# Prologue of a tuned kernel: text rows loaded in two pieces, patches in halves, rows of two batches computed directly, the order of loads and of GpSimd work changed

## The chip, the core and the metric

The kernel runs on one core of a Trainium2 chip. The metric is the device time in microseconds of one execution; the median of three runs stands for a kernel. The profile is of one further execution.

The engines are TensorE (PE in the rows; PEld is its loading of weights), VectorE (DVE), ScalarE (ACT), GpSimd (POOL) and SyncE (SP). SyncE only issues loads and stores here; ScalarE and GpSimd issue some too. An engine works through its own instructions in order and waits on semaphores for the others.

## What is computed

Eight images are cut into 36 patches of 768 numbers each and projected to 192; 128 rows of text follow them, so each of the 8 batches has 164 rows of 192. An attention with 12 heads and a routed feed-forward net of 16 experts are added. All is float32.

```
h = patches @ proj_w.T + proj_b + pos          # (8, 36, 192)
h = concat([h, txt], axis=1)                   # (8, 164, 192)
xn = layernorm(layernorm(h)) * ln_w
Q  = xn[:, None] * W_qk[None, :, None]         # 12 heads, Q is also K
A  = softmax(causal(Q @ Q.T / sqrt(192)))
o  = A @ (xn - mean(wte, axis=0))              # wte: 50257 x 192
h  = h + (o / row_number).reshape(8, 164, 12*192) @ W_o.T
h  = h + moe(layernorm(h))                     # top-1 of 16 experts, 64 rows each at most
```

The mean over the table wte (38.6 MB) is needed only at the end of the attention. The kernel adds the table up beside the attention.

## The kernel before

**Rows and batches.** Each batch of 164 rows is kept as 128 rows (36 patches and 92 of text, in H, row on partition) and 36 rows of text (in hB). Batch 0 has a stretch of its own before the loop. `iteration(b)` of every engine then finishes batch b and starts batch b + 1: TensorE computes the last two score groups of b (text rows, all heads), transposes z of b + 1, computes the values of b in four groups `value(b, 0..3)`, and between them the scores of b + 1 in groups `score(b+1, 0..2)` of 4 heads and the projection `project(b, ...)` of b with W_o. There are seven such iterations (0 to 6); behind them stand the last batch and the feed-forward part, which the change leaves alone.

**One batch on the other engines.** VectorE normalises: `variances` (BN stats), a power on GpSimd (`rsqrt`), a Newton step (`factors`), then `z(b)` makes zA and zB. TensorE transposes them, ScalarE copies the result (zT). GpSimd's `weigh` multiplies zT by the squared weights of each head into AwA (groups 0 to 2) and AwB (text rows, 3); for batch 0 ScalarE and VectorE make the halves with k = 0. After the scores VectorE takes row maxima (`row_max`), ScalarE the exponentials (`exps`), VectorE a factor per row (`row_factor`), and GpSimd multiplies (`normalise`). TensorE transposes P, ScalarE copies it to a rounded high part (`t_copy`), VectorE makes the rest (`t_low`), and the values use both. `value_low` does the same for z. `o_copy` and `e_copy` empty the value banks, `residual` adds the projection to H.

**The prologue.** SyncE loads the projection weights, the patches, the text rows (txtA, partitions 36 to 127, in one load), waits for these and for some constants, and then issues wo_attn, the first two chunks of wte, txtBp and further loads. ScalarE's queue carries the constants: cst, txtB, position and bias, wqk, lnw and then lncol, flnw, wrt and flc. TensorE keeps warm with 14 products of ones, computes embT = patches^T for batches 0 and 1 first (`embed`, in bT[1]), ScalarE copies it, and `token_transpose(j)` gives the patch rows of two batches at a time; VectorE's `add_patches(j)` adds the position and writes H. Then follow the other six batches in the same way, with 12 more warming products around the transposes of z.

**The table.** 28 chunks of 1.34 MB. Six are loaded plain by SyncE (`plain_loads`, one per batch) and summed by VectorE (`plain_sum`). The other 22 go through two buffers: the first two by plain loads, the other 20 by loads that add in memory, which GpSimd issues (`add_wte`), three per iteration for iterations 0 to 5. `add_wte` waits until the earlier load into its buffer has landed. Everything that GpSimd has to do after it waits too. In the loop, the three adds stand before the weighing of groups 0 and 1, before that of group 2, and before `normalise(b+1, (1,))`.

**Order.** It is written by hand on every engine; there is no planner. `mat` is a set of constants that ScalarE converts to bfloat16 after its iteration 1 and TensorE uses after batch 7.

## Time and profile before

| | us |
|---|---|
| median of three runs | 373.03 (372.75 to 373.41) |
| the profiled execution | 372.14 |
| its span | 370.4 |
| TensorE busy in the span | 332.7 (90%) |
| VectorE, GpSimd, ScalarE busy | 219.9, 169.0, 127.9 |

The span is cut into the prologue (up to 37.8 us, where TensorE transposes z of batch 1), batch 0 (to 71.6), the loop, and from 203 us the end of the attention and the experts. TensorE is the busiest engine, so its idle stretches are where to look; in the chain of work that ended last TensorE has 39%, loads 14% and GpSimd 14% of the span.

In a row of the timeline the columns are: start in us, duration in us, engine, line of the kernel, operation, what is written <- what is read, shape, and in brackets how long the engine stood idle before it and who ended that. "x16" means that 16 instructions are merged in the row. One float32 matmul shows as two.

### The profile page before, as it was taken

To read this page: it belongs to the slowest core of one execution; us is meant where nothing else is said; L and a number is where in the kernel's file an instruction comes from. 1 tells how busy PE (TensorE), PEld (TensorE's weight loads), DVE (VectorE), ACT (ScalarE), POOL (GpSimd) and SP (SyncE) were. 2 spreads that over 40 slices of the span, in tenths; PEclk is the share of its full clock that TensorE was granted. 3 is DMA by queue.
4 is the path that set the end of the run, shared out by engine and by line. 5 is a ranking of instruction groups with operands and counts; after the bars stand their busy time and mean duration, and the time that the engine had idled before them with its cause. 6 is when DMAs were issued, how large, how long until landed. Compare 5 with 4: busy or idle time off the path is not lost.

```text
span 370.4 us, 6796 instructions
## 1 busy us (share of the span) xinstructions
PE 332.7 (90%) x2352; PEld 306.4 (83%) x2352; DVE 219.9 (59%) x546; ACT 127.9 (35%) x438; POOL 169.0 (46%) x181
## 2 busy tenths in 40 slices
PE   5886779999799899899899898999949999999992
PEld 1866679989699799799798798999824999999991
DVE  1479638678669679578588888656476222222221
ACT  2065423644643453454436004545720111111110
POOL 3067375583574763862953501450562134444321
PEclk9899889999999999999999999999998999999997
DMA  7399999899799899799797999900223599999930
GB/s 226 114 419 341 215 213 212 236 177 210 221 196 213 225 199 239 191 199 271 162 198 155 295 229 237 230 11 0 84 101 93 165 276 276 273 265 272 273 93 15
DMA packets 20176, 74.29 MB, mean 201 GB/s; under 512 B 3388, under 2 KB 9021, under 8 KB 18874
## 3 DMA queue, kind: packets, MB, share of 16 engines
q0 software_dynamic: 7344, 30.57, 40.8%
q1 hardware_dynamic: 9898, 40.40, 36.8%
q10 hardware_dynamic: 2912, 3.04, 2.9%
q8 instruction: 12, 0.20, 0.2%
q14 instruction: 10, 0.08, 0.1%
HBM read 66.12 MB, written 9.25 MB: 203 GB/s over the span
## 4 chain that ended last, share of the span: by engine, by line
PE 39%; issue 18%; DMA 14%; POOL 14%; DVE 8%; ACT 3%; POOLq 1%; SPq 0%; DVEq 0%; ACTq 0%
PE bO L1198 18%; DMA wbuf<-in_wte 11%; PE bE L1198 10%; PE bS L1198 5%; PE bJ L1198 4%; POOL AwA L390 4%; DMA H<-in_txtA 4%; POOL PA L416 3%; POOL wbuf L401 3%; POOL AwB L390 2%; ACT PA L552 2%; POOL PB L416 1%; DVE negmax L791 1%; PE bT L1544 1%; DVE PTB0L L808 1%
## 5 line engine op out<-in xcount | busy, mean ns | idle before, releaser
L552 ACT ACTIVATE PA<-bS,negmax 128x128 f32<-128x128 f32 x96 | 33.9, 366 | 85.2 <-DVE negmax L791 85.2
L416 POOL TENSOR_TENSOR PA<-PA,rn 128x512 f32<-128x512 f32 x24 | 25.8, 1075 | 64.3 <-DVE rn L803 64.3
L390 POOL TENSOR_TENSOR AwA<-zT,w 96x512 f32<-96x512 f32 x45 | 53.4, 1514 | 3.3 <-ACT zT L534 3.3
L1198 PE MATMUL bJ<-wo_sb,oTA 128*128 128x192 f32 x288 | 51.4, 328 | 0.0
L1198 PEld LDWEIGHTS bS<-zT,AwA 96*128 96x128 f32 x384 | 48.0, 197 | 1.1
L1198 PE MATMUL bS<-zT,AwA 96*128 96x128 f32 x384 | 48.2, 280 | 0.0
L1198 PEld LDWEIGHTS bJ<-wo_sb,oTA 128*128 128x128 f32 x288 | 46.2, 190 | 0.0
L1198 PE MATMUL bO<-PA,wx 96*128 96x112 f32 x384 | 45.4, 275 | 0.5 <-DVE PA L1171 0.5
L1198 PEld LDWEIGHTS bO<-PA,wx 96*128 96x128 f32 x384 | 44.9, 192 | 0.7 <-DVE PA L1171 0.7
L463 POOL DMA_INDIRECT out<-PA,yrow x16 | 15.0, 940 | 56.1 <-DVE PA L1187 56.1
L689 ACT ACTIVATE AwA<-bO 128x448 f32<-128x448 f32 x16 | 8.7, 543 | 78.4 <-PE bO L1198 52.8
L1198 PE MATMUL bE<-wx,AwA 128*112 128x192 f32 x192 | 33.9, 326 | 0.0
L827 DVE TENSOR_REDUCE wx<-wx 128x672 f32 (+1 forms) x24 | 31.5, 1314 | 0.0
L401 POOL DMA_DIRECT2D wbuf<-in_wte x20 | 27.3, 1363 | 7.7 <-DMA wbuf<-in_wte 6.2
L1198 PEld LDWEIGHTS bE<-wx,AwA 128*112 128x112 f32 x192 | 30.4, 177 | 0.0
L1180 DVE TENSOR_SCALAR AwA<-bO 128x224 f32<-128x224 f32 x16 | 6.3, 391 | 36.7 <-PE bO L1198 34.5
L791 DVE TENSOR_REDUCE negmax<-bS 128x4 f32<-128x512 f32 x24 | 16.5, 687 | 13.7 <-PE bS L1198 13.5
L416 POOL TENSOR_TENSOR PB<-PB,rn 108x328 f32<-108x328 f32 x16 | 11.7, 733 | 28.1 <-DVE rn L803 27.3
L570 ACT ACTIVATE oTA<-bO,lncol 128x512 f32<-128x512 f32 x24 | 16.6, 690 | 13.0 <-PE bO L1198 12.9
L1198 PE MATMUL bS<-zT,AwB 96*108 96x164 f32 x128 | 20.3, 302 | 0.0
L458 POOL DMA_INDIRECT dispatched<-pay,posI x11 | 12.3, 1122 | 16.3 <-ACT pay L616 12.1
L552 ACT ACTIVATION_READ_ACCUMULATOR PA<-bS,negmax 128x1 f32 x96 | 19.5, 203 | 0.0
(247 smaller groups left out, 690.9 us busy)
## 6 DMA issues: line engine op xcount, KB each, us to landing
wbuf<-in_wte POOLq DMA_DIRECT2D x20, 1344.0 KB, 13.0
wx<-in_wi SPq DMA_DIRECT2D x16, 576.0 KB
wx<-in_wo SPq DMA_DIRECT2D x16, 576.0 KB
wx<-in_wte SPq DMA_DIRECT2D x6, 1344.0 KB, 8.5
dispatched<-zeros SPq DMA_DIRECT2D x7, 675.5 KB, 10.3
wbuf<-in_wte SPq DMA_DIRECT2D x2, 1344.0 KB, 12.1
AwA<-dispatched ACTq DMA_DIRECT2D x14, 168.9 KB
wo_sb<-in_wo_attn SPq DMA_DIRECT2D x1, 1728.0 KB, 6.9
```

The source lines that it names most:

```text
L390: nc.gpsimd.tensor_tensor(o, zT[:, k, ss].unsqueeze(1).to_broadcast(list(o.shape)), w2[:, k, hs].unsqueeze(2).to_broadcast(list(o.shape)), ...
L401: pool.dma_start(wchunk[s], wv[:, ds(c, 1), :].rearrange("p c x -> p (c x)"), accum_op=ALU.add, max_dma_last_dim=WR * EMB * 4 // 2).then_i ...
L416: nc.gpsimd.tensor_tensor(t, t, q.unsqueeze(2).to_broadcast(list(t.shape)), ALU.mult).then_inc(p_ready, 1)
L458: nc.gpsimd.indirect_dma_start(out=xd[:, :], out_offset=bass.IndirectOffsetOnAxis(ap=posI[0:n, j:j + 1], axis=0), in_=pay[0:n, j, :], in_o ...
L463: nc.gpsimd.indirect_dma_start(out=out[:, :], out_offset=bass.IndirectOffsetOnAxis(ap=idx, axis=0), in_=rows, in_offset=None, bounds_check ...
L552: last = nc.scalar.activation(PA[:, h, :], bank[:, j * SA:(j + 1) * SA], ACT.Exp, bias=negmax[:, h:h + 1], accum_out=lsum[:, h:h + 1])
L570: nc.scalar.activation(dst, src, ACT.Copy, scale=lncol[:, 0:1]).then_inc(o_used, 1)
L689: nc.scalar.activation(hT[:, 0:4, :], bO[0][:, 0:4 * T].rearrange("p (c n) -> p c n", c=4), ACT.Relu).then_inc(h0_ready, 1)
L791: nc.vector.tensor_reduce(negmax[:, 4 * r:4 * r + 4], bS[r % 2][:, :].rearrange("p (h s) -> p h s", h=4), X, ALU.max, negate=True).then_in ...
L827: nc.vector.tensor_reduce(psums.rearrange("p (n e) -> p n e", e=EMB)[:, ds(b, 1), q].rearrange("p n e -> p (n e)"), plain.rearrange("p (r ...
L1180: nc.vector.tensor_scalar(hT[:, 4:6, :], bO[1][:, 0:2 * T].rearrange("p (c n) -> p c n", c=2), 0.0, None, ALU.max).then_inc(h1_ready, 1)
L1198: return nc.tensor.matmul(o, l, r, start=start, stop=stop, skip_group_check=True)
```

## The change

- The text rows of txtA are loaded as 80 and 12 partitions instead of 92; txtBp is loaded right behind them, before SyncE waits.
- Patches and projection weights come in two halves of three slices each (pat_in, pat2_in), to other buffers (parts of wx[1] and wx[3]), as does embT.
- Rows of batches 0 and 1 are computed directly (`embed_rows`, patches x weights); the other six go by `embed` and `token_transpose` as before, the second half of `embed` after the transposes of z of batch 0 and the transposes after score groups 0 and 1. The 12 warming products there are gone.
- SyncE also waits for w2 and ln; the first two table chunks are issued before wo_attn, and mat is loaded after all plain chunks. ScalarE issues its late constants after the patches have landed, and converts mat in iteration 6.
- VectorE's variances and factors of batches 2 to 7, and three of the adds of patches, move back into and behind the scores of batch 0.
- GpSimd weighs z of the next batch (groups 0 and 1) before the first add of an iteration; the second add comes after `normalise(b+1, (0,))`, the third after the weighing of the text rows. Iterations 0 and 1 stand outside its loop.

```diff
-            sp.dma_start(pw_sb, projw).then_inc(pat_in, 16)
-            sp.dma_start(pat_sb, patches).then_inc(pat_in, 16)
-            sp.dma_start(H[IMG:128, 0:NBATCH, :], txtA).then_inc(txt_in, 16)
+            for part, arrived in ((slice(0, 3), pat_in), (slice(3, 6), pat2_in)):
+                sp.dma_start(pw_sb[:, part, :], projw[:, part, :]).then_inc(arrived, 16)
+                sp.dma_start(pat_sb[:, part, :], patches[:, part, :]).then_inc(arrived, 16)
+            for p0, p1 in ((IMG, 116), (116, 128)):
+                sp.dma_start(H[p0:p1, 0:NBATCH, :], txtA[p0 - IMG:p1 - IMG]).then_inc(txt_in, 16)
+            sp.dma_start(H[0:BP, NBATCH:SLOTS, :], txtBp).then_inc(late_in, 16)
...
-            sp.wait_ge(txt_in, 16)
-            sp.dma_start(wo_sb[:, :, :], wo_attn).then_inc(wo_in, 16)
+            sp.wait_ge(w_in, 32)
+            sp.wait_ge(txt_in, 32)
             for s in range(WBUF):
                 sp.dma_start(wchunk[s], wv[:, s, :]).then_inc(wte_first, 16)
-            sp.dma_start(H[0:BP, NBATCH:SLOTS, :], txtBp).then_inc(late_in, 16)
+            sp.dma_start(wo_sb[:, :, :], wo_attn).then_inc(wo_in, 16)
...
+            plain_loads(sp)
             sp.dma_start(mat32, cst2_d[:, C_MAT:NCST2]).then_inc(mat_in, 16)
-            plain_loads(sp)
...
             pool.wait_ge(w2_ready, 1)
-            weigh(0, 1, (1,), range(3))
-            rsqrt(rstd[:, :, 2:NBATCH], nmr[:, :, 2:NBATCH], 2)
-            weigh(0, 1, (1,), (3,))
-            normalise(0, range(1))
+            weigh(0, 1, (1,))
             add_wte(2, 0, 0)
-            normalise(0, range(1, 2))
             add_wte(3, 1, 0)
-            normalise(0, range(2, 3))
+            normalise(0, range(3))
...
                 normalise(b, range(3, SPR))
-                for k in range(4):
-                    if r is not None and k < 3:
-                        add_wte_nth(i, r + k)
-                    if k == 0:
-                        weigh(b + 1, t_before(b, "z") + 1, (0, 1), (0, 1))
-                    elif k == 1:
-                        weigh(b + 1, t_before(b, "z") + 1, (0, 1), (2,))
-                        normalise(b + 1, (0,))
-                    elif k == 2:
-                        normalise(b + 1, (1,))
-                        weigh(b + 1, t_before(b, "z") + 1, (0, 1), (3,))
-                    else:
-                        normalise(b + 1, (2,))
+                n = t_before(b, "z") + 1
+                weigh(b + 1, n, (0, 1), (0, 1))
+                if r is not None:
+                    add_wte_nth(i, r)
+                weigh(b + 1, n, (0, 1), (2,))
+                normalise(b + 1, (0,))
+                if is0(b):
+                    rsqrt(rstd[:, :, 2:NBATCH], nmr[:, :, 2:NBATCH], 2)
+                if r is not None:
+                    add_wte_nth(i, r + 1)
+                normalise(b + 1, (1,))
+                weigh(b + 1, n, (0, 1), (3,))
+                if r is not None:
+                    add_wte_nth(i, r + 2)
+                normalise(b + 1, (2,))
...
             dve.wait_ge(vz_ready, 3)
             z(0)
-            for j in range(1, 4):
-                add_patches(j)
-            variances(2, NBATCH)
-            row_max(0, 0)
             dve.wait_ge(t_used, 1)
             nc.vector.tensor_tensor(AwB[:, 0, :, :], ...)
+            row_max(0, 0)
             row_max(0, 1)
             row_factor(0, 0)
-            value_low(0)
+            for j in range(2, 5):
+                add_patches(j)
             row_factor(0, 1)
             row_max(0, 2)
+            value_low(0)
             dve.wait_ge(t_ready, 1)
             z(1)
             row_factor(0, 2)
-            factors(2, NBATCH, 2)
...
                 e_copy(b, 2)
+                if is0(b):
+                    variances(2, NBATCH)
                 plain_sum(b, 0)
...
                 dve.wait_ge(t_ready, t_before(b, "z") + 1)
+                if is0(b):
+                    factors(2, NBATCH, 2)
                 z(b + 2)
...
-            embed(bT[1][0:EC, 0:EF], 0, 0, EF)
-            embed(bT[1][0:EC, 128:128 + EF], 1, 0, EF).then_inc(emb_ready, 1)
+            embed_rows(0, 0, 3)
+            embed_rows(1, 0, 3)
+            pe.wait_ge(pat2_in, 32)
+            embed_rows(0, 3, 6)
+            embed_rows(1, 3, 6)
             embed(bO[0][0:EC, EF:NBATCH * IMG], 0, EF, NBATCH * IMG).then_inc(emb_ready, 1)
...
-            stay_warm(bS[0], 6)
             z_transpose(0, 0)
-            stay_warm(bS[0], 6)
+            embed(bO[1][0:EC, EF:NBATCH * IMG], 1, EF, NBATCH * IMG).then_inc(emb_ready, 1)
             pe.wait_ge(bf_ready, 3)
-            for r in range(3):
-                score(0, r, r < 2)
+            score(0, 0, True)
+            score(0, 1, True)
+            pe.wait_ge(embT_ready, 2)
+            for j in range(1, 4):
+                token_transpose(j)
+            score(0, 2)
```

## Rows read from the trace of the kernel before

**Rows 1.** Stretches: busy time of each engine, granted clock, DMA share, GB/s.
```profile
71.60:98.40 26.80, 25.15 (x179) 23.30 (x178) 19.57 (x38) 14.07 (x49) 16.08 (x18) 1.00 0.94 205
98.40:124.50 26.10, 24.39 (x175) 22.77 (x174) 19.30 (x37) 11.84 (x47) 15.96 (x16) 1.00 0.95 211
```

**Rows 2.** Chain of work in order of time; then one stretch as in rows 1.
```profile
1.76 13.91 DMA H<-in_txtA
...
10.00:11.00 1.00, 0.78 (x9) 0.79 (x10) 0.97 (x10) 0.00 (x0) 0.00 (x0) 1.00 0.26 106
```

**Rows 3.** Timeline of the prologue, TensorE and VectorE; then one load, KB, landing.
```profile
10.22 3.26 PE L1198 MATMUL bT<-AwA 128*96 128x72 f32 x24 [4.29 <-DMA AwA<-in_patches]
...
13.83 0.18 DVE L757 TENSOR_TENSOR w<-w,ln 96x24 f32<-96x24 f32 x1 [2.50 <-DMA ln<-in_lnw]
...
16.69 0.55 DVE L743 TENSOR_TENSOR H<-bT,cS 36x384 f32<-36x384 f32 x1 [2.25 <-PE bT L1219]
...
20.83 0.37 DVE L785 TENSOR_SCALAR zB<-hB,rstd,nmr 36x192 f32<-36x192 f32 x1
...
ln<-in_lnw ACTq DMA_DIRECT2D x1, 0.8 KB, 10.3
```

**Rows 4.** Timeline from the first scores to the transposes of z(1).
```profile
22.87 1.66 DVE L763 BATCH_NORM_STATS2 st<-H 128x6 f32<-128x192 f32 x6
...
26.33 0.69 DVE L791 TENSOR_REDUCE negmax<-bS 128x4 f32<-128x512 f32 x1 [0.47 <-PE bS L1198]
...
31.86 2.30 DVE L783 TENSOR_SCALAR zA<-H,rstd,nmr 128x192 f32<-128x192 f32 x1
...
33.34 1.76 POOL L401 DMA_DIRECT2D wbuf<-in_wte  x1
...
34.09 0.36 DVE L785 TENSOR_SCALAR zB<-hB,rstd,nmr 36x192 f32<-36x192 f32 x1
...
34.71 0.17 DVE L730 TENSOR_TENSOR nwz<-rstd 128x12 f32<-128x12 f32 x1
...
36.86 0.19 DVE L886 TENSOR_TENSOR wr_sb<-wr_sb,flc 96x32 f32<-96x32 f32 x1
...
37.84 0.32 PE L1241 MATMUL bT<-cst,zA 128*96 128x128 f32 x1 [1.96 <-DVE PTAL L808]
```

**Rows 5.** Timeline of iteration 0, GpSimd, TensorE, VectorE; last the score of iteration 1.
```profile
44.92 1.21 POOL L401 DMA_DIRECT2D wbuf<-in_wte  x1 [3.12 <-DMA wbuf<-in_wte]
...
48.29 0.38 PE L1198 MATMUL bS<-maskA,idb 128*128 128x512 bf16 x1 [3.37 <-issue]
48.50 3.37 PE L1198 MATMUL bS<-zT,AwA 96*128 96x128 f32 x16
...
51.91 0.69 DVE L791 TENSOR_REDUCE negmax<-bS 128x4 f32<-128x512 f32 x1 [5.28 <-PE bS L1198]
...
75.19 1.95 PE L1198 MATMUL bS<-zT,AwA 96*128 96x128 f32 x16
```

**Rows 6.** One iteration of the loop; then a wait: us, times, longest.
```profile
124.50 1.20 POOL L401 DMA_DIRECT2D wbuf<-in_wte  x1
125.27 4.49 POOL L390 TENSOR_TENSOR AwA<-zT,w 96x512 f32<-96x512 f32 x4
...
136.99 2.12 PE L1198 MATMUL bJ<-wo_sb,oTA 128*128 128x192 f32 x12
...
PE bS L1198 <- POOL AwA L390: 4.1, 5, 0.9
```

**Rows 7.** Timeline of ScalarE in the second iteration.
```profile
91.18 1.92 ACT L608 ACTIVATE mat<-pay 128x2048 bf16<-128x2048 f32 x1
```

**Rows 8.** GpSimd's normalising and third add; then the adding loads, us to landing.
```profile
118.62 1.04 POOL L416 TENSOR_TENSOR PA<-PA,rn 128x512 f32<-128x512 f32 x1 [3.73 <-DVE rn L803]
...
134.98 1.21 POOL L401 DMA_DIRECT2D wbuf<-in_wte  x1
...
wbuf<-in_wte POOLq DMA_DIRECT2D x20, 1344.0 KB, 13.0
```

73 lines of the change are left out of this document (37 added, 36 removed).

## The prediction

> **What bounds the kernel now.** I read three views, in this order. First the busy time by stage [rows 1]: in a batch of the running loop (98.4 to 124.5 us) TensorE is busy 24.39 of 26.10 us, so the loop goes at TensorE's pace but for 1.7 us. Then the chain of waits from the start, with the DMA share beside it [rows 2]: the first long link is the load of the text rows, issued at 1.76 and landed at 15.67, while in 10 to 11 us (and alike up to 15) the 16 DMA engines are at 0.26 of their time, 106 GB/s. That is four engines' worth; one load is still under way on a quarter of them. Last the waits of each engine in batch 0 and in the loop [rows 3 to 6]. The end of the run is set by TensorE from batch 1 on, so what counts is (a) how early TensorE gets through batch 0 and (b) each hole it has in the loop.
>
> The working is in old times: a term is how much earlier TensorE's stream stands against its old place. It is made against the profiled execution, 372.14 us with a span of 370.4; the 1.74 around the span stay, and the median of the runs, 373.03, is 0.9 above it, so the gain is taken from 373.03 at the end.
>
> **Term 1, up to z of batch 0.** Now: the patches (one load) let TensorE start at 10.22, it makes embT for two batches, ScalarE copies it, four transposes give the rows, VectorE adds the position at 16.69, and zB ends at 20.83 + 0.37 = 21.20 [rows 3]. The direct product patches x weights needs no copy and no transposes. It is 12 matmuls with 192 columns; such matmuls take 0.33 us each in the loop (six of them, 12 halves in the profile, in 2.12 us, [rows 6]), so 4.0 us at the full clock, half of it on the first three slices, which come in before the second half. The second half is the end of the same 1.44 MB and lands about when the patches land now, 10.2, or somewhat before, since the late constants of ScalarE's queue (109 KB) now wait behind it and the text no longer shares its engines: I take 9.8. Then six matmuls, 2.0 us: rows of batch 0 at 10.8, of batch 1 at 11.8. The text (480 KB on 80 partitions) follows at the rate of a full set of engines: 106 GB/s x 4 for 480 + 72 KB is 1.3 us, so about 11.2. What is late next is VectorE: it is idle 2.50 us for the load ln and makes w at 13.83 [rows 3]. If ln still lands then, VectorE reaches the two adds at 14.43, ends them (two of 0.4) at 15.2, and z ends 3.95 later as now (17.24 to 21.20), at 19.2: gain 2.0. If ln lands with the rest at 11.3, adds end at 12.6 and z at 16.6: gain 4.6. A load of 0.8 KB that takes 10.3 us while its neighbours in the queue take 5 to 7 is held up by something on its engines, and the text load is the only thing there until 15.67; I take 4.0, ends 2.0 and 4.8.
> The Trainium skill (DMA: Bandwidth & Descriptors, "Why a DMA increments its semaphore by 16 and not by 1") says that a load is spread over the largest number up to 16 that divides its partitions, and that its semaphore write comes after all earlier writes of the same engine. By it 92 rows use 4 engines, 80 use 16, 12 use 12, and ln waits behind the text; the 0.26 share agrees, and the sum by it would be 4.6 instead of 4.0.
>
> **Term 2, from z to the transposes of z of batch 1 (21.20 to 37.84, [rows 4]).** On VectorE 2.99 us of variances (22.87 to 25.86, where the wait of 0.47 before the first row maximum begins) leave their place, worth nothing there because of that wait. The block between z(1) and the first t_low, 34.71 to 37.05, moves into and behind batch 0: 2.3 us, on the path, because TensorE waits 1.96 us at 37.84 for exactly that t_low. Added: the three adds of patches (0.55 each, 1.7) between row maximum 1 and row maximum 2. Between the exponentials of a row group VectorE waits for ScalarE, which hides most of them; I put 0.3; the copy emb_copy(1) on ScalarE costs 0.35 before the first exponentials. The second embed product (2.2 us full clock, 4 at half) stands before the first score, which comes 2.0 us after the z transposes anyway for want of weighed z: 0.2 to 2. GpSimd's four weighings run on without the power of the other batches in between, and its first adds of the table no longer wait with a row in front: the two chunks come ahead of wo_attn, issued about 12.5 instead of 16.1, 2.9 MB at 0.4 MB/us, in by about 21.5, about when GpSimd comes to them. And zA(1), 2.30 us beside GpSimd's work, may be 0.4 or stay. Sum: 2.3 + up to 1.9 - 0.3 - 0.35 - 0.2 to 2: 0.5 to 3; I take 2.0.
>
> **Term 3, the first values (37.84 to 44.92).** TensorE runs there at half speed after its idle stretch: a score of 16 halves right after the hole takes 3.37, in the loop 1.95 [rows 5]. Without the 1.96 us hole the same work takes some 5.6 instead of 7.1: 1.4 (0 to 1.6).
>
> **Term 4, the hole before the score of batch 1.** GpSimd waits 3.12 us for a table chunk (41.80 to 44.92) before it issues the add; only then does it weigh z, and TensorE idles 3.37 us until 48.29 [rows 5]. With the weighing in front it starts at 41.8 and is done with the first group 2.0 us later, in these old times at 43.8 and earlier still with the terms above: the whole hole goes, and 1.42 us of slow clock on the score, together 4.8, up to the value of the last group. But the variances of six batches, 2.99 us, now stand on VectorE between the last e_copy and the row maximum of batch 1; so far VectorE had 5.28 us to spare there, which the hole gave it [rows 5]. Without the hole: e_copy ends at x, variances x + 3.0, plain_sum 1.3, maximum 0.7, exponentials 1.5, two copies and differences of P 1.9: x + 8.4, whereas TensorE, leaving its score at x + 1, gets to that value at x + 5.5 or so. It waits 2.9 there, a new hole. Net 4.8 - 2.9 = 1.9 (0.9 to 4.7). After such a hole the clock falls again, now on the stretch behind it: -0.8 (0 to -1.6), in which the factors of the other batches (2.4 with a slow step) are too; they stand before z(2), and its row maximum had 2 us of slack to the end of the batch.
>
> **Term 5, the loop.** In a batch the add is issued at 124.50 and the weighing starts 0.77 later, at 125.27; TensorE waits 0.8 for the weighed z, 4.1 us in 5 batches [rows 6]. With the add behind the first four weighings 0.77 of it goes: 5 x 0.75 = 3.8 (0 to 4.1). The moved adds: the second stays at its place, the third goes behind the weighing of the text rows, just where VectorE makes z(b+2). TensorE's other waits of 0.2 to 0.3 stay. Term 6: the conversion of mat, 1.92 us on ScalarE [rows 7], made its batch 26.8 us long instead of 26.1 [rows 1]; in its new place ScalarE is idle: 0.65 (0 to 0.7). Its load of 1 MB goes behind the last plain chunk, tens of us ahead of its use; the table's last chunks get some 3 us later by it. From there to the end nothing moves but by the shift.
>
> **Sum:** 4.0 + 2.0 + 1.4 + 1.9 - 0.8 + 3.8 + 0.65 = 12.95; 373.03 - 12.95 = 360.1. All lower ends give 1.8, all upper ones 18.9; they don't fall together.
>
> **Rival A: the moved add costs VectorE what TensorE gains (the loop gives 0).** The chain into TensorE's 0.80 wait runs through VectorE without slack: e_copy, value_low, z, maxima, t_low, exponentials, GpSimd's normalising. Two-source operations of VectorE stretch when GpSimd is at work: zA took 2.30, where zB with the same columns takes 0.36, in a stretch with an add and a normalising [rows 4]. If an add of 1.2 us does that alone, z is 0.7 later and the 0.77 are given back: 12.95 - 3.8 = 9.2, 363.9. Against it: zB at 34.09 took its usual 0.36 while an add was being issued (33.34 to 35.10) [rows 4].
> The Trainium skill (SBUF — State Buffer, the box on "DVE blocks DMA") tells of one port pair of VectorE and GpSimd which is locked for a whole instruction, descriptors of GpSimd's DMAs included. Taken both ways it is this rival, 363.9; the row of zB speaks against it, that of zA for it.
>
> **Rival B: the prologue gives little.** ln or the 12 rows still land near 13.8, and TensorE, with its warming matmuls gone, falls to half clock before the z transposes: term 1 is 2.0, term 2 is 0.5 to 1: 12.95 - 2.0 - 1.3 = 9.7, 363.4. For it: TensorE idled 4.29 us before 10.22 [rows 3] and would be idle some 3 before z. If splitting the text doesn't do what it says at all (both pieces land at 15.7) term 1 is 0.5: 365.
>
> **Rival C, slower: GpSimd stuck behind the table.** The third add follows the first, into the same buffer, by 12.5 us (now 10.5), and behind it stands the normalising of the third round, on which TensorE's transposes wait; GpSimd is idle 3.73 us before it [rows 8], and TensorE comes to it about 3 us after it is done, by my reading of the order. An add lands 13.0 us after its issue [rows 8]; the DMA share of a batch is 0.95 [rows 1] and batches get shorter, so it may grow. Above 19.2 us each further one costs six batches 1 us: slower than before from 21.4 us on; at 23 it is 22.8 - 12.95 = 10 slower, 383. Against it: the bytes of a batch stay the same, and now the third add follows the first after 10.5 us (134.98 less 124.50) without a wait for it.
>
> **Chances.** As forecast 0.60 (356 to 363), A 0.15, B 0.17 (both 361 to 367), text split without effect 0.04, C 0.03, no change 0.01. The range 355.5 to 367.0 holds the first three but for their edges, some 0.85. About 0.2% is what a measurement here tells from no change. Faster 0.96, same 0.01, slower 0.03.
>
> **What the new profile would show.** Text landed near 11, w made near 12, z(0) finished near 17; the transposes of z(1) near 32; no wait of TensorE for weighed z in batch 0, but 2 to 3 us before its last value; "TensorE waits for GpSimd's weighed z" near 0.2 us in all, VectorE's zA in the loop about 0.4 (else A); a batch of 25.4 us without exception; the loop's end 12 to 13 us earlier and the rest unchanged. A wrong size of the hole in batch 0 and the clock behind it is what is likeliest to spoil the number.

## The result, and the profile after

| | us |
|---|---|
| before, median beside these runs | 373.22 |
| after, median of four runs | 377.16 (372.82, 376.93, 377.40, 382.04) |
| ratio to before | 1.008 (95%: 1.005 to 1.012) |
| forecast | 360.1 (355.5 to 367.0) |
| the profiled execution of after, its span | 372.82, 371.0 |

The change makes the kernel slower by 0.8%, where 12.95 us of gain were forecast. The run of 382.04 fell in a slower state of the chip; the ratio and all medians below leave such runs out, which makes this one 376.93. The profiled execution is the shortest of the four; v1_after_again below shows what a longer one loses.

From the page of after: TensorE's busy time, and the shares of the chain of work that ended last:

```profile
PE 333.8 (90%) x2336; PEld 305.3 (82%) x2336; DVE 218.3 (59%) x547; ACT 126.4 (34%) x437; POOL 167.9 (45%) x181
...
PE 46%; DVE 21%; DMA 18%; ACT 7%; issue 5%; ACTq 1%; DVEq 1%; POOLq 0%; POOL 0%
```

TensorE is busy about as long as before (332.7 us), so what was to be gained is still in its idle stretches and in matmuls at a lower clock. GpSimd, with 14% of the chain in before, has left it, and 15% of the span are now one kind of load, the plain chunks of the table (`DMA wx<-in_wte`).

The waits of after between 60 and 205 us (who waited for whom, us in total, times, longest) hold two that before has not:

```profile
DVE wx L833 <- DMA wx<-in_wte: 8.2, 5, 2.0
PE bO L1206 <- DVE PTB1L L814: 8.0, 5, 2.0
```

TensorE's wait for GpSimd's weighed z [rows 6] is gone, as forecast. In its place VectorE waits in every iteration for the plain chunk of the table, and TensorE, for as long, for VectorE. The reason is in the tile of that load. First before, then after (us from issue to landing):

```profile
DMA to landing us min/median/max: 7.6/8.4/9.4
```
```profile
DMA to landing us min/median/max: 11.1/11.3/11.7
```

The chain of work that ended last, in after, from the first to the second of these loads:

```profile
61.87 1.24 DVE wx L833
63.12 11.07 DMA wx<-in_wte
...
75.60 0.69 DVE negmax L797
...
87.72 0.59 DVE negmax L797
88.32 1.25 DVE wx L833
89.58 11.26 DMA wx<-in_wte
```

This is a ring, a closed loop through one buffer. SyncE issues the next load only when VectorE has summed the last quarter of the chunk before (88.32 + 1.25), and VectorE can't go on in the next batch before the load has landed. In the next batch the first quarter starts at 100.99 and the last ends at 116.2, 15.2 us later. With 11.4 us from issue to first use the ring is 26.65 us long, and this is what an iteration takes (26.70 on average). GpSimd's timeline of after shows the pace at the normalising of the text rows, once per iteration:

```profile
68.43 1.57 POOL L420 TENSOR_TENSOR PB<-PB,rn 108x328 f32<-108x328 f32 x2 [3.43 <-DVE rn L809]
94.77 1.57 POOL L420 TENSOR_TENSOR PB<-PB,rn 108x328 f32<-108x328 f32 x2 [3.32 <-DVE rn L809]
...
201.93 1.57 POOL L420 TENSOR_TENSOR PB<-PB,rn 108x328 f32<-108x328 f32 x2 [3.33 <-DVE rn L809]
```

The same rows of before stand at 69.86 and 201.53. I use this event as a clock below and call it "text rows of batch 1" (68.43) and "of batch 6" (201.93). So after enters the loop 1.43 us earlier than before, and leaves it 0.40 later: 133.50 us for five iterations instead of 131.67.

The prologue, TensorE and VectorE of after:

```profile
13.56 0.18 DVE L762 TENSOR_TENSOR w<-w,ln 96x24 f32<-96x24 f32 x1 [3.86 <-DMA ln<-in_lnw]
18.39 0.37 DVE L791 TENSOR_SCALAR zB<-hB,rstd,nmr 36x192 f32<-36x192 f32 x1
33.99 0.27 PE L1252 MATMUL bT<-cst,zA 128*96 128x128 f32 x1
40.21 0.39 PE L1206 MATMUL bS<-maskA,idb 128*128 128x512 bf16 x1
```

And iteration 0 of after, in which the lead that the prologue has won is lost (VectorE, then TensorE):

```profile
40.80 1.65 DVE L768 BATCH_NORM_STATS2 st<-H 128x6 f32<-128x192 f32 x6
42.49 0.51 DVE L771 BATCH_NORM_AGGREGATE mv<-st 128x2 f32<-128x6 f32 x6
43.03 2.00 DVE L773 TENSOR_SCALAR nmr<-mv 128x12 f32<-128x12 f32 x1
...
49.71 0.59 DVE L814 TENSOR_TENSOR PTB1L<-bT,PTB1H 36x432 fp32r<-36x432 f32 x1
```
```profile
50.45 0.70 PE L1206 MATMUL bO<-PTB0H,vAH 128*128 128x432 f32 x1 [4.00 <-DVE PTB1L L814]
...
55.27 2.63 PE L1206 MATMUL bJ<-wo_sb,oTA 128*128 128x192 f32 x12
```

The score of batch 1 starts at 40.21 without a wait; in before it is at 48.29 [rows 5], 8.1 us later. Before the last group of values (50.45) TensorE stands idle for 4.00 us, and the 12 projection halves behind that take 2.63 us instead of 2.12.

### The profile page after: what moved, and what is told of

Its sections match the earlier page's. It is cut to its first block, busy times and chain, and to the rows that moved or that the text cites. A ratio compares the mean times of both kernels' runs of the same rounds, so it can differ in the third digit from the quotient of the medians.

```text
span 371.0 us, 6757 instructions
## 1 busy us (share of the span) xinstructions
PE 333.8 (90%) x2336; PEld 305.3 (82%) x2336; DVE 218.3 (59%) x547; ACT 126.4 (34%) x437; POOL 167.9 (45%) x181
## 4 chain that ended last, share of the span: by engine, by line
PE 46%; DVE 21%; DMA 18%; ACT 7%; issue 5%; ACTq 1%; DVEq 1%; POOLq 0%; POOL 0%
PE bO L1206 21%; DMA wx<-in_wte 15%; PE bE L1206 12%; PE bJ L1206 6%; PE bS L1206 4%; ACT PA L557 3%; DMA ln<-in_lnw 3%; DVE negmax L797 2%; DVE wx L833 2%; DVE vAL L826 2%; DVE vBL L824 2%; DVE vBL L826 1%; DVE PTB0L L814 1%; DVE PTB1L L814 1%; DVE PTAL L814 1%
## 5 line engine op out<-in xcount | busy, mean ns | idle before, releaser
L420 POOL TENSOR_TENSOR PA<-PA,rn 128x512 f32<-128x512 f32 x24 | 24.8, 1034 | 77.8 <-DVE rn L809 77.8
L394 POOL TENSOR_TENSOR AwA<-zT,w 96x512 f32<-96x512 f32 x45 | 48.4, 1161 | 3.5 <-ACT zT L539 3.5
L1206 PEld LDWEIGHTS bS<-zT,AwA 96*128 96x128 f32 x384 | 46.8, 192 | 1.2
L1206 PE MATMUL bS<-zT,AwA 96*128 96x128 f32 x384 | 46.8, 275 | 0.0
L405 POOL DMA_DIRECT2D wbuf<-in_wte x20 | 24.1, 1230 | 0.0
## 6 DMA issues: line engine op xcount, KB each, us to landing
wbuf<-in_wte POOLq DMA_DIRECT2D x20, 1344.0 KB, 11.2
wx<-in_wi SPq DMA_DIRECT2D x16, 576.0 KB, 11.5
wx<-in_wte SPq DMA_DIRECT2D x6, 1344.0 KB, 11.3
wo_sb<-in_wo_attn SPq DMA_DIRECT2D x1, 1728.0 KB, 12.3
```

What stands on the lines that cost most here:

```text
L394: nc.gpsimd.tensor_tensor(o, zT[:, k, ss].unsqueeze(1).to_broadcast(list(o.shape)), w2[:, k, hs].unsqueeze(2).to_broadcast(list(o.shape)), ...
L405: pool.dma_start(wchunk[s], wv[:, ds(c, 1), :].rearrange("p c x -> p (c x)"), accum_op=ALU.add, max_dma_last_dim=WR * EMB * 4 // 2).then_i ...
L420: nc.gpsimd.tensor_tensor(t, t, q.unsqueeze(2).to_broadcast(list(t.shape)), ALU.mult).then_inc(p_ready, 1)
L1206: return nc.tensor.matmul(o, l, r, start=start, stop=stop, skip_group_check=True)
```

## Experiments on the ring (the loop)

**Theory.** The ring of one buffer sets the pace of after. It does so because the third add of the table now stands close in front of the plain load (issued at 86.44, the plain load at 89.58; in before they are some 9 us apart, 82.15 and 91.0) and shares the DMA engines with it. **Rivals.** VectorE stretched by adds (rival A), or contention for bytes that no buffer cures.

**x1_two_plain.** After, with two buffers for plain chunks in turn:

```diff
-        plain = wx[0][:, :]
+        plain = (wx[0][:, :], wx[2][:, :])
...
-                    if n:
-                        sp.wait_ge(plain_used, 4 * n)
-                    sp.dma_start(plain, ...).then_inc(plain_in, 16)
+                    if n > 1:
+                        sp.wait_ge(plain_used, 4 * (n - 1))
+                    sp.dma_start(plain[n % 2], ...).then_inc(plain_in[n % 2], 16)
```

> The changed kernel, but with two buffers for the plain chunks of the table (the second in wx[2]), so that a chunk is loaded a batch ahead; VectorE's loop is written out in pairs for that. Theory T (the moved adds lengthen the plain load from 8.4 to 11.3 us, and VectorE waits 8.2 us for it in 5 iterations, with TensorE behind it): the wait is gone, an iteration takes 25.1 us instead of 26.7, and the time is 373 - 8 = 365 (363 to 367). Rival R (the loads as such are the bound, any gain before them is given back there): the wait moves to GpSimd's adds or to the end of the table, an iteration stays above 26, and the time is 370 to 375.

Measured: 364.66, ratio to before 0.981 (0.976 to 0.987). Its waits have no row for the plain chunk, though the loads take as long as in after:

```profile
DMA to landing us min/median/max: 11.4/11.5/11.7
```
```profile
68.10 1.57 POOL L421 TENSOR_TENSOR PB<-PB,rn 108x328 f32<-108x328 f32 x2 [3.30 <-DVE rn L810]
...
194.84 1.57 POOL L421 TENSOR_TENSOR PB<-PB,rn 108x328 f32<-108x328 f32 x2 [3.32 <-DVE rn L810]
```

126.74 us for five iterations, 25.35 each. The loads are as slow as before, only the wait goes. Between the profiled executions (372.82 and 364.87) this gives 8.0 us, of which 6.8 are in these five iterations; between the medians it is 12 us, measured on two chips (10 by the two ratios to before). In this loop the first quarter is wanted 9.8 us after the last one of the batch before is done (88.17 to 97.94). That is what a ring of one buffer allows for the load at this pace; a load of 11.4 us exceeds it by 1.6, and 5 times 1.6 is about the 8.2 us of the wait.

**x3_before_third.** The kernel before, with nothing but the third add moved behind the weighing of the text rows (from k = 2 to k = 3):

```diff
-                    if r is not None and k < 3:
-                        add_wte_nth(i, r + k)
+                    if r is not None and k != 2:
+                        add_wte_nth(i, r + min(k, 2))
```

> The kernel before with one thing moved: the third add of each iteration goes from before the normalising of round 1 to behind the weighing of the text rows. Theory T: the plain load takes 10.5 to 11.5 us instead of 8.4, VectorE waits for it 1 to 1.5 us in each of 5 iterations, 26.7 us an iteration: 373.2 + 2.5 = 375.7 (374.5 to 378). Rival R: a place in the order changes nothing, 373.

Measured: 375.58, ratio 1.009 (1.006 to 1.013).

```profile
DVE wx L827 <- DMA wx<-in_wte: 2.9, 4, 1.9
```
```profile
DMA to landing us min/median/max: 9.9/10.1/10.9
```

The place of this one add, which I had costed at nothing, is enough: the plain load lands 1.7 us later, VectorE waits, and the kernel before becomes some 3 us slower (375.58 against 372.44 beside it; in the profile five iterations take 133.43 us instead of 131.67). It doesn't explain all of the 11.3 us in after. There the second add is later too (80.28, 9.3 us before the plain load; in before 14.7), so that by the median time to landing (11.2 us; in before 13.3) two adds are under way when the plain load is issued, where in before it is one. What this is worth wasn't tried by itself.

**x2_old_adds.** After, with the adds of iterations 1 to 5 back in front of the weighings:

```diff
+                if r is not None and not is0(b):
+                    add_wte_nth(i, r)
                 weigh(b + 1, n, (0, 1), (0, 1))
                 if r is not None:
-                    add_wte_nth(i, r)
+                    add_wte_nth(i, r if is0(b) else r + 1)
                 weigh(b + 1, n, (0, 1), (2,))
                 normalise(b + 1, (0,))
...
-                    add_wte_nth(i, r + 1)
+                    add_wte_nth(i, r + 1 if is0(b) else r + 2)
...
-                if r is not None:
+                if r is not None and is0(b):
                     add_wte_nth(i, r + 2)
```

> The changed kernel with the adds of iterations 1 to 5 back in their old places; iteration 0 keeps the weighing in front. Theory T: plain load 8.4 us, no wait of VectorE, an iteration of 26.15 us as before; the 3.0 us that TensorE has gained at the end of iteration 0 and 0.65 of the conversion stay: 369.5 (368.5 to 371). Rival R: no different from the changed kernel, 373 to 377.

Measured: 372.05, ratio 0.997 (0.994 to 1.001). The plain loads land in 8.1 to 8.3 us but for the first (11.6), which follows iteration 0 with its third add in the new place. The old wait is back,

```profile
PE bS L1208 <- POOL AwA L394: 4.3, 5, 1.0
```

and an iteration takes 26.3 us. The mechanism is as expected, the time 2.6 above my figure of 369.5. Iteration 0 has the same hole of 4.00 us as in after (text rows of batch 1 at 68.62), and of the 1.45 us by which the profiled execution leaves the loop earlier than before (200.08) nothing is left at its end; where they go stands behind y3_text_one, at the end of the experiments.

**x4_one_first.** After, with the adds one weighing earlier each, so that the third is issued well ahead of the plain load (the conditions `if r is not None` are left out here):

```diff
-                weigh(b + 1, n, (0, 1), (0, 1))
+                weigh(b + 1, n, (0, 1), (0,))
                 add_wte_nth(i, r)
+                weigh(b + 1, n, (0, 1), (1,))
+                add_wte_nth(i, r + 1)
                 weigh(b + 1, n, (0, 1), (2,))
                 normalise(b + 1, (0,))
-                add_wte_nth(i, r + 1)
+                add_wte_nth(i, r + 2)
                 normalise(b + 1, (1,))
                 weigh(b + 1, n, (0, 1), (3,))
-                add_wte_nth(i, r + 2)
```

> The changed kernel with another order on GpSimd, in all iterations: weigh group 0, add, weigh group 1, add, weigh group 2, normalise round 0, add, normalise round 1, weigh the text rows, normalise round 2; that is before's order but for one weighing ahead of the first add. Theory T: the adds are as early against the plain load as in the kernel before, it lands in 8 to 9 us, VectorE doesn't wait, TensorE has the first group 0.77 us earlier: 25.3 us an iteration and 364 to 367 in all. Rival R: 370 to 375. Should the gain of the loop come from nothing but the adds' place, this equals the run with two plain buffers within 1.5 us.

Measured: 369.52, ratio 0.993 (0.990 to 0.997), above the 364 to 367 expected. The plain loads land in 8.2 us, so that wait is gone, but another engine now waits:

```profile
POOL wbuf L405 <- DMA wbuf<-in_wte: 14.5, 5, 3.0
```

This is rival C of the prediction in a mild form: the third add (105.44) comes before the first one, into the same buffer (94.89), has landed, and GpSimd stands in front of it for 2.9 us with its normalising behind. An iteration takes 26.4 us. So of the two orders tried, one is too early (GpSimd waits) and one too late (the plain load is late): the old places were a compromise with 1.9 us of slack (10.3 us from the last use of the buffer to the next first one, less 8.4 of load).

**z3_before_plain.** The kernel before with two plain buffers, nothing else:

> The kernel before with two plain buffers in turn, and nothing else. Theory (the second buffer only takes away a wait that the new order of GpSimd makes; before, VectorE does not wait for plain loads): same as before, 372.6, with 26.1 us an iteration. Rival (the second buffer gives something by itself, since the plain load can go at any time): 369 or less, with under 25.6 us an iteration.

Measured: 375.66, ratio 1.007 (1.005 to 1.010). The loop keeps 26.3 us an iteration (131.46 us for five, before 131.67), near what was expected, but the kernel is 3 us slower, which I had not. The place is the first add of iteration 0, in [rows 5] after 3.12 us of waiting; GpSimd in z3_before_plain:

```profile
48.07 1.21 POOL L402 DMA_DIRECT2D wbuf<-in_wte  x1 [5.95 <-DMA wbuf<-in_wte]
```

A second plain chunk (1.34 MB) is now asked for at the start, ahead of the load that GpSimd waits for. That load, issued at 31.82, takes over 15 us instead of 12.8; the add is 3.2 us later than in before (48.07, 44.92), the text rows of batch 1 are 4.2 later (74.02, 69.86), and those of batch 6 are 4.0 later (205.48). Before that load the prologue is at most 0.5 us late (31.82, in before 31.36), so the second chunk is the likely cause; it wasn't tried alone. A second buffer isn't free where an engine waits for the loads that it overtakes.

**y4_before_pool_plain.** z3_before_plain with the new order of GpSimd's iterations; the prologue is that of before:

> The kernel before with GpSimd's new order in the iterations and two plain buffers, and nothing of the prologue changed. Theory T: the loop gives 5 x 0.75 and batch 0 the hole of 3.37 us and some slow clock: 372.4 - 3.8 - 4 = 364.6 (363 to 367), so that nearly all that the changed kernel with two buffers gains comes from this and little from the prologue. If the prologue carried it instead: 368 to 371.

Measured: 365.21, ratio 0.979 (0.975 to 0.983), as the theory had it; text rows of batch 1 at 65.74, of batch 6 at 193.02. The late table chunk no longer matters, since the weighing stands in front of the add. With this order and two buffers the new prologue adds next to nothing (364.66 against 365.21). By the text rows it even loses: x1_two_plain has them at 68.10 and 194.84, 2.4 and 1.8 us later than here. The next section asks why.

**v1_after_again.** The kernel after, unchanged, on another chip.

> The kernel after once more, on another chip, beside the kernel before. Its four times were 372.82 (the profiled one), 376.93, 377.40 and 382.04, so the profile shows the shortest of them, and what the others lost has not been seen. Theory (the ring of one plain buffer sets the pace, and its length hangs on how long a plain load takes to land beside the adds): median between 375 and 378; in a profiled execution of some 377 the iteration is 27.2 to 27.5 us instead of 26.7 and the plain loads land in about 12 us. Rival (the loop is the same and the time is lost at the end, in the experts): iterations of 26.7, and the experts' stretch 4 us longer.

Measured: 376.37, ratio 1.011 (1.008 to 1.014), as the theory had it; the profiled execution took 375.19. Its chain:

```profile
116.28 1.24 DVE wx L834
117.54 12.26 DMA wx<-in_wte
...
143.90 1.25 DVE wx L834
145.17 11.80 DMA wx<-in_wte
```

The plain loads take 11.5 to 12.3 us, VectorE waits 10.4 us for them, and five iterations take 137.27 us, 27.45 each, against 26.70 in the first profile of after. The text rows of batch 6 come 2.5 us later, the whole execution is 2.4 us longer. So this longer run loses its time in the loop, where the ring is: once a load is on the path, its spread is the kernel's. (The first of the five iterations takes 28.45 us; in it TensorE also runs at a granted clock of 0.66 from 79 to 84 us, behind a hole of 1.78.) The runs of 377 and more weren't profiled.

## Experiments on the prologue and iteration 0

**z2_prologue_only.** After, with GpSimd's iterations (0 included) in the order of before, one plain buffer:

```diff
-                weigh(b + 1, n, (0, 1), (0, 1))
-                if r is not None:
-                    add_wte_nth(i, r)
...
+                for k in range(4):
+                    if r is not None and k < 3:
+                        add_wte_nth(i, r + k)
```

> The kernel after, but in its iterations GpSimd has the order of the kernel before again (each add in front of a weighing or a normalising), with one plain buffer. It says what the prologue of the change is worth by itself. Theory (y4_before_pool_plain against x1_two_plain: the prologue is worth less than 1 us): 372 to 373.3 beside 373. The last plain loads land in 8.5 us, GpSimd's wait for the table chunk in batch 0 and TensorE's hole of 3 us behind it are back. Rival (the prologue's 3 us of earlier TensorE work, seen in the kernel after, come through once the loop does not take them back): 369 to 370.

Measured: 368.52, ratio 0.990 (0.985 to 0.995), nearest to the rival and somewhat below its 369: by itself the prologue, with the new place of mat, is worth 4.2 us. TensorE and GpSimd in iteration 0:

```profile
49.50 0.44 PE L1206 MATMUL bO<-PTB0H,vAH 128*128 128x432 f32 x1 [1.11 <-DVE PTB1L L814]
```
```profile
65.73 1.57 POOL L420 TENSOR_TENSOR PB<-PB,rn 108x328 f32<-108x328 f32 x2 [3.43 <-DVE rn L809]
```

The hole before the value is 1.11 us instead of 4.00, no slow clock behind it, and batch 1 is there at 65.73, 2.7 us earlier than in after, although its score starts 2.0 later (42.17). x2_old_adds differs from this kernel in iteration 0 alone: 68.62 and 372.05. The new order in iteration 0, which I had counted as the end of a hole, costs about 3 us beside the new place of the variances (2.9 by the text rows, 3.5 by the medians).

**y1_var_late.** x1_two_plain, with the variances and their power later in iteration 0:

```diff
             def iteration(b, par, turn):          # VectorE
...
                 e_copy(b, 2)
-                if is0(b):
-                    variances(2, NBATCH)
                 plain_sum(b, 0, par, turn)
...
                 plain_sum(b, 2, par, turn)
+                if is0(b):
+                    variances(2, NBATCH)
...
                 normalise(b + 1, (0,))            # GpSimd
-                if is0(b):
-                    rsqrt(rstd[:, :, 2:NBATCH], nmr[:, :, 2:NBATCH], 2)
...
                 normalise(b + 1, (1,))
+                if is0(b):
+                    rsqrt(rstd[:, :, 2:NBATCH], nmr[:, :, 2:NBATCH], 2)
```

> Changed kernel with two plain buffers, and the variances of batches 2 to 7 (4.2 us on VectorE there, 40.8 to 45.0) moved from before the row maximum of batch 1 to before the last e_copy of batch 0, where VectorE waits 3.4 us for TensorE; GpSimd's power goes behind the normalising of round 1. Theory V (the variances make TensorE's hole of 4.00 us in batch 0 and the 2.3 us of half clock behind it): hole under 1 us, batch 1 starts 4 to 6 us earlier, 364.7 - 5 = 360 (358.5 to 362). Rival (VectorE's chain up to the start of batch 1 gives it back): the hole goes, but the first loop iteration starts no earlier, 364.

Measured: 364.52, ratio 0.980 (0.976 to 0.984). This is the rival's time, but not what the rival said would happen. The hole of 4.34 us in x1_two_plain is gone (0.26 is left), and batch 1 does come earlier, by 3.0 us:

```profile
65.06 1.57 POOL L421 TENSOR_TENSOR PB<-PB,rn 108x328 f32<-108x328 f32 x2 [3.30 <-DVE rn L810]
```

It isn't the 4 to 6 us of the theory, since in the waits of 40 to 62 us stands

```profile
DVE nwz L735 <- POOL rstd L384: 2.1, 1, 2.1
```

VectorE now waits for the power before z(2), and TensorE as long for the exponentials (2.29 us at 60.21). At the end of the loop 1.9 of the 3.0 us are left (192.92 against 194.84). All but 0.2 of these go behind the loop, where the 26 warming products ahead of the experts run at a granted clock that differs from profile to profile. First x1_two_plain, then y1_var_late:

```profile
271.24 5.78 PE L1209 MATMUL bJ<-ones 128*128 128x512 bf16 x26 [1.51 <-DVE nbI L1165]
```
```profile
269.30 8.37 PE L1209 MATMUL bJ<-ones 128*128 128x512 bf16 x26 [1.50 <-DVE nbI L1165]
```

That the two kernels take the same time (364.87 and 364.66 in their profiles) is thus an accident of the clock there, and no sign that the variances don't matter.

**z1_best.** y1_var_late, with the power in its old place again, and VectorE's product of the router's weights taken from behind iteration 0 to where VectorE has time:

```diff
                 normalise(b + 1, (0,))            # GpSimd
+                if is0(b):
+                    rsqrt(rstd[:, :, 2:NBATCH], nmr[:, :, 2:NBATCH], 2)
...
                 plain_sum(b, 1, par, turn)        # VectorE
+                if is0(b):
+                    dve.wait_ge(late_in, 16 * 5)
+                    link(nc.vector.tensor_tensor(wr_sb[:, :, :], ...))
```

> The kernel after, with the two plain buffers of x1_two_plain; VectorE's variances of batches 2 to 7 stand before the last e_copy of batch 0 as in y1_var_late, but GpSimd takes their power ahead of the first normalising of batch 1, and VectorE scales the router's weights one step later. Theory (what y1_var_late lost was VectorE's wait of 2.15 us for the power): that wait goes, batch 1 starts some 1.5 to 2 us earlier than in x1_two_plain, which had 364.66, and this stays to the end of the loop: 361.5, between 360 and 363.5. Rival (time won in batch 0 is given back at the end, where the experts' first blocks wait for work that does not move): 364.5, with the warming products of 8 us or more ahead of the experts, as in y1_var_late.

Measured: 361.70, ratio 0.970 (0.966 to 0.974), the fastest of all and 4% under the kernel after; the theory had 361.5.

```profile
64.54 1.57 POOL L421 TENSOR_TENSOR PB<-PB,rn 108x328 f32<-108x328 f32 x2 [2.18 <-DVE rn L810]
...
191.19 1.57 POOL L421 TENSOR_TENSOR PB<-PB,rn 108x328 f32<-108x328 f32 x2 [3.32 <-DVE rn L810]
```

VectorE's wait for the power is 1.17 us instead of 2.15, not quite gone. Batch 1 is there 3.6 us earlier than in x1_two_plain, of which y1_var_late already had 3.0. The variances in the wrong place are what had eaten most of the prologue's gain. In the right place the prologue is worth 3.5 us beside the new order too (against the 365.21 of y4_before_pool_plain); in the profiled executions 1.8 of this are there at the text rows of batch 6 (191.19, 193.02), and the other 1.8 are in the warming products (7.11 and 8.64 us) and just ahead of them.

**v2_iter0_old.** x1_two_plain, with the adds in the old places in iteration 0 alone:

```diff
+                if is0(b):
+                    add_wte_nth(i, r)
                 weigh(b + 1, n, (0, 1), (0, 1))
+                if is0(b):
+                    add_wte_nth(i, r + 1)
                 weigh(b + 1, n, (0, 1), (2,))
                 normalise(b + 1, (0,))
+                if is0(b):
+                    add_wte_nth(i, r + 2)
```

> The kernel x1_two_plain (after with two plain buffers), but in iteration 0 alone GpSimd has its adds in the old places, in front of the weighings. x1_two_plain had 364.66, with 4.34 us of hole before the value of batch 0 and the text rows' normalising of batch 1 at 68.10; z2_prologue_only, with the old places everywhere, has 1.11 us of hole, and that normalising at 65.73. Theory (the new order in iteration 0 brings TensorE's score early and so makes a long hole behind it, which lowers the clock; with an add in front there are two short ones): the normalising at 65.7, then 25.4 us an iteration, 362.3, between 361.5 and 363.5. Rival (the earlier start is lost in the tail or to the table's chunks, which GpSimd now has to wait for in batch 1): 364 to 365.

Measured: 367.53, ratio 0.986 (0.982 to 0.990), text rows of batch 1 at 70.20 instead of 65.7. Neither case holds: the add in front of the weighing waits, as in z3_before_plain, for a load that the second plain chunk stands ahead of:

```profile
42.23 1.20 POOL L406 DMA_DIRECT2D wbuf<-in_wte  x1 [2.95 <-DMA wbuf<-in_wte]
```

In z2_prologue_only, with one plain buffer, that wait is 0.79. The second buffer and the old order don't go together in iteration 0, the new order and the early variances don't either; of the combinations tried z1_best has the good one.

## Experiments on the loads of the prologue

**y2_ln_first.** x1_two_plain, with w2 and ln issued first on ScalarE's queue (in the diff, ahead of cst):

```diff
+            for dst, src in ((w2[:], wqk), (ln96[:], lnw)):
+                act.dma_start(dst, src).then_inc(w_in, 16)
```

> Changed kernel with two plain buffers, and ScalarE issues the two small loads w and ln first instead of fifth and sixth. In the changed kernel VectorE waits 3.86 us for ln (until 13.47) and SyncE's table loads wait for it as well. Theory L (ln is late because it stands behind other transfers): it lands by 8, z of batch 0 is done near 17.2 instead of 18.8, 364.7 - 1.5 = 363.2. Rival (a load of 8 byte pieces takes its 10 us wherever it stands, or its end is reported only when the engines are empty): ln lands after 11, 364.7.

Measured: 366.71, worse by 2 than the 364.66 of x1_two_plain. The first step of theory L holds: ln lands 3.8 us after its issue instead of 10.1, and VectorE no longer waits for it. But the other loads come later. VectorE begins with the text rows of hB at 11.63 instead of 6.59, and TensorE waits for the second half of the patches,

```profile
12.41 1.82 PE L1209 MATMUL bT<-wx 128*36 128x192 f32 x5 [4.16 <-DMA wx<-in_patches]
```

and zB starts at 19.93 instead of 18.53. So the times of both cases fall, and with them the rival's claim that ln takes 10 us wherever it stands.

**y3_text_one.** x1_two_plain, with the text rows in one load of 92 partitions:

```diff
-            for p0, p1 in ((IMG, 116), (116, 128)):
+            for p0, p1 in ((IMG, 128),):
```

> Changed kernel with two plain buffers, and the text rows in one load of 92 partitions as in the kernel before. Shows what the split is worth. If the split is what brings the text early (theory): it lands near 15.5 instead of before 13, z of batch 0 is 0.7 to 1.5 later, and 364.7 + 1 = 365.7. If the gain of the prologue is from elsewhere: 364.7.

Measured: 367.6, worse by 3 than x1_two_plain, of which the profile shows 0.8 at z (zB at 19.37 instead of 18.53). VectorE's timeline:

```profile
11.86 0.18 DVE L763 TENSOR_TENSOR w<-w,ln 96x24 f32<-96x24 f32 x1 [1.99 <-DMA ln<-in_lnw]
...
15.81 0.62 DVE L769 BATCH_NORM_STATS2 st<-H 128x6 f32<-128x192 f32 x2 [2.71 <-DMA H<-in_txtA]
```

The text is what is late (15.8), as in [rows 2], and VectorE has ln 1.8 us earlier than with the text split (11.86 here, 13.69 in x1_two_plain). So splitting the text moves ln back, where the forecast had it come forward. The Trainium skill (DMA: Bandwidth & Descriptors, "Queues, rings and completion order") says that a load's semaphore write lands only after every earlier write of the same DMA engine. The forecast read from it that ln waits for the whole text load; the trace doesn't agree with that reading, for ln is used at 11.86 here and at 13.83 in before, while the text lands at 15.8 and 15.67. Which of the other writes ln waits for, no run here shows.

**What lies behind the loop.** The profiled executions settle where the rest of these 2 and 3 us goes. From the text rows of batch 6 to the 26 warming products it is 76.4 us in x1_two_plain, y1_var_late, y2_ln_first, y3_text_one and z1_best alike (76.6 in y4_before_pool_plain), and from the end of these products to the end of the run 87.0 to 87.9. The products themselves take 5.78, 8.37, 7.07, 8.39, 7.11 and 8.64 us. In y3_text_one this makes 1.9 of the 3.2 us that its profile is longer, in y2_ln_first 0.4 of 1.1; the loop's end is 1.3 and 0.7 us later. The same products take 8.36 us in x2_old_adds and 7.20 in before. A difference of a us or two between two medians can thus come from there, and the text rows are the better measure of what a change in the prologue is worth.

## Why the prediction was wrong, step by step

Against [rows 3 to 6], in the profiled execution of after:

| term | forecast | measured | seen at |
|---|---|---|---|
| 1, z of batch 0 | 4.0 (2.0 to 4.8) | 2.44 | end of zB: 21.20, now 18.76 |
| 2, to the transposes of z(1) | 2.0 (0.5 to 3) | 1.41 | 37.84, now 33.99 |
| 3, first values | 1.4 (0 to 1.6) | 0.86 | TensorE free for the score of batch 1: 44.92, now 40.21 |
| 4, from there to batch 1 | 1.9 - 0.8 = 1.1 (lower end 0.9 - 1.6 = -0.7) | -3.28 | text rows of batch 1: 69.86, now 68.43 |
| 5 and 6, the loop with mat | 3.8 + 0.65 | -1.83 | 131.67 us, now 133.50 |
| the end | 0 | -0.3 | 372.14 less 201.53, 372.82 less 201.93 |

The sum of the measured column is -0.7: 372.14 to 372.82. Of the 13.6 us between forecast and profile, terms 5 and 6 have 6.3, term 4 has 4.4, and terms 1 to 3 have 2.7. By the medians the kernel is some 3 us further off still, since the profiled execution was the shortest; v1_after_again shows the loop as the place for this.

**Terms 1 to 3** were right in kind and each too large; together 4.71 instead of 7.4. In term 1 the upper bound rested on ln being held up by the text. [Rows 2, 3] already spoke against it: ln is used at 13.83, the text lands only at 15.67. The term came out near its lower bound, as rival B had it; TensorE's half clock at the transposes of z(0) (0.45 us for the first, 0.27 in before) is of that rival too.

**Term 4** named the right mechanism, a new hole before the last value of batch 0 since six batches' variances stand in VectorE's way, and sized it too small. I had 8.4 us from the last e_copy to the rest of P; it took 9.5 (40.80 to 50.30). The difference is one operation on 128 x 12 numbers: nmr took 2.00 us, where in before it took 0.76, and ended at 45.03, as GpSimd's weighing beside it did (44.99), which the change had just moved there. In z1_best, away from it, it takes 0.17. Thus the hole was 4.00 instead of 2.9. Behind it TensorE ran at the lower of its levels: from 50.45 to the projection at 55.27 it needs 4.8 us for what takes 2.6 in before (56.20 to 58.79), and 0.5 more in the projection. That is 2.7 us instead of the 0.8 I took (the bound was 1.6). The stretch from 49 to 60 us of after, then of z2_prologue_only (busy time of each engine, granted clock, DMA share, GB/s):

```profile
49.00:60.00 11.00, 9.55 (x49) 9.31 (x50) 7.35 (x16) 3.13 (x14) 8.08 (x7) 0.69 0.64 117
```
```profile
49.00:60.00 11.00, 10.50 (x75) 10.36 (x76) 9.59 (x19) 3.62 (x18) 7.22 (x6) 1.00 1.05 212
```

And VectorE, late by the hole, reaches z(2) with the five operations of the factors in front (59.53 to 60.57); I had given them 2 us of slack, which by then was used up. At the projection of iteration 0 with 16 halves TensorE's lead was still 3.0 us (59.74 against 62.75), at the text rows of batch 1 it is 1.43. About 1.1 us of this loss is VectorE's product of the router's weights: the change moved it from batch 0, where it took 0.19 us [rows 4], to the end of iteration 0, where it takes 1.00 (64.06) and the differences of P wait behind it (65.29). No term had it.

**Term 5** is the step that failed. Its mechanism holds (x1_two_plain: five iterations in 126.74, so 4.2 us besides mat), but the third add "goes behind the weighing of the text rows, just where VectorE makes z(b+2)" was weighed against VectorE's and GpSimd's time alone, and its effect on the plain load was put at nothing without a reason. I asked who waits behind the add, not whose load stands behind it on the DMA engines. The plain load has the same size, is issued 3.1 us after the third add instead of 9, and lands in 11.3 us instead of 8.4. VectorE and TensorE wait 8.2 and 8.0 us for it, and the loop, forecast 4.45 us shorter, is 1.83 longer. I never read the landing of that load, nor the time from one chunk's last use to the next one's first (91.0 to 101.30 in before, 10.3 us), which would have shown that 2 us more were enough to close the ring. The forecast also says that the second add stays at its place; by the diff it moves too, from before the weighing of group 2 to behind `normalise(b+1, (0,))`.

**Term 6** held: in z2_prologue_only the iteration with the old conversion takes 26.15 us, in before 26.89, so 0.74 instead of 0.65.

**Rival A** did not come: in the loop zA takes 0.40 and zB 0.53 us, in before 0.38 and 0.37. The Trainium skill (SBUF — State Buffer, the box on "DVE blocks DMA") tells of the lock in one direction, an instruction of VectorE that keeps GpSimd from writing the descriptors of a DMA; rival A took it in the other direction too. Beside the issues of adds the rows give VectorE 0.2 us a batch more; what was long in VectorE stood beside GpSimd's products (nmr, below). **Rival C**, GpSimd stuck at the third add, came in x4_one_first, not here. That the end of the loop could be slower than before for the sake of a load that the diff doesn't name was in none of my cases; all of them had one mechanism on GpSimd, VectorE or TensorE, and the DMA share of 0.95 [rows 1] stood only for the adds.

The medians, taken one edit at a time: from before to z2_prologue_only (prologue and mat) -4.2, from there to x2_old_adds (new order in iteration 0) +3.5, from there to after (new order in the loop, one buffer; 376.8 over both chips) +4.8. They lead from 373 to 377 by construction; what they say is the size of each step.

**Open:** what holds ln for 10 us in its old place, where it takes 3.8 us at the head of its queue. Why the 26 warming products take from 5.8 to 8.6 us from profile to profile. How much of the 11.3 us is due to the second add. A plain load issued at some other moment, which would have tried the contention without a second buffer, wasn't tried.

## What to carry to other kernels

A load into a single buffer, whose issue waits for the last use and whose landing is waited for at the next first use, is a ring; write down its length (landing plus the time from first to last use) beside the period of the loop before anything on the same DMA engines is moved, since a load that never showed as a wait can be within 2 us of being one. Where a hole is closed, ask what stood in its shadow, and move that first: with the variances in the same place TensorE's hole was 1.11 us in one order of GpSimd and 4.0 in another. Changes that go together should be priced together: by the medians the prologue was worth 4.2, 0.5 or 3.5 us, depending on two others. And compare at an event inside the run as well as at its end: y1_var_late was 1.9 us ahead where the loop ends, and its time didn't show it.

## What the runs showed of the hardware

- A plain load of 1.34 MB, issued 3 us after an adding load of the same size instead of 9 us, lands in 11.3 us instead of 8.4 with the full new order (after), in 10.1 with that add alone moved (x3_before_third).
- An operation of VectorE on 128 x 12 numbers took 0.17, 0.86, 2.00 and 3.02 us in four kernels (z1_best, z2_prologue_only, after, v2_iter0_old). In the last three it began beside GpSimd's products of 96 x 512 and ended 0.04 to 0.05 us after the row of them did (44.09 and 44.05; 45.03 and 44.99; 47.51 and 47.46), however many products were left; the BN stats ahead of it, beside the same products, kept their 1.65 us.
- The same 26 bf16 products of ones (128 x 512) ahead of the experts took from 5.78 us (x1_two_plain, x4_one_first) to 8.64 (y4_before_pool_plain), behind an idle stretch of 1.5 us each time. The granted clock during them was 1.00 in x1_two_plain and 0.68 in y1_var_late (8.37 us).
- An idle stretch of TensorE of 4.0 us (after, before 50.45) was followed by half-rate rows for some 5 us, the granted clock from 49 to 60 us being 0.69. The length of the stretch alone doesn't tell this in advance. Before the transposes of z(0), 2.83 us idle (v1_after_again) and 3.96 (z2_prologue_only) were followed by rows at the full rate within one instruction (0.32 and 0.31, then 0.27 us), 3.83 (z1_best) and 3.91 (after) by rows at half rate (0.45, then 0.42). In z2_prologue_only the granted clock then fell all the same, to 0.50 from 20 to 22 us, and in before 1.96 us idle (before 37.84) were followed by 0.63 from 38 to 40 us and 0.52 from 40 to 42.
